# Gate and up products with the weights stationary, so that the hidden values come out transposed

## What is computed

```python
def h_bitlinear(x, w):
    xq = act_quant(fwht(x))      # per-token scale 127 / max|.|, rounded
    wq = weight_quant(w)         # -1, 0, 1 times one scale
    return jnp.einsum('bsh,oh->bso', xq, wq)
gate = h_bitlinear(hidden_states, w_gate)     # 512 -> 2048
up = h_bitlinear(hidden_states, w_up)         # 512 -> 2048
return h_bitlinear(jax.nn.silu(gate) * up, w_down)   # 2048 -> 512
...
x = x + _L0_xattn_ref(_layernorm(x, axis=-1), ...)
x = x + _L0_ffn_ref(_layernorm(x, axis=-1), ...)
```

## Time and profile before

| | |
|---|---|
| median of 3 runs | 1400.6 us (1399.08 to 1401.05) |
| profiled execution, its time | 1399.5 us |
| its span in the trace | 1397.7 us |
| PE busy | 1375.2 us, 98% of the span |
| DVE, ACT, POOL busy | 936.5, 938.9, 449.5 us |
| feed-forward part | from about 1012 us to the end |
| starts of the 13 gate and up groups | 1022.30, 1051.39, then 29.17 apart until 1343.05, last 1371.80 |

### The profile page before, as it was taken

One profiled execution on the slowest core, in us unless ns is written; L12 is line 12 of the kernel. 1 busy time (PEld: TensorE's weight loads), 2 busy tenths in 40 slices (PEclk: granted clock), 3 DMA queues, 4 the chain that ended last, 5 costly groups with the idle time before them and its releaser, 6 DMA issues. The chain is left out here.

```text
span 1397.7 us, 25965 instructions
## 1 busy us (share of the span) xinstructions
PE 1375.2 (98%) x8419; PEld 1181.4 (85%) x8419; DVE 936.5 (67%) x2403; ACT 938.9 (67%) x2072; POOL 449.5 (32%) x325
## 2 busy tenths in 40 slices
PE   9999999999999999999999999999999999999998
PEld 9889868999999999999999999998866677766775
DVE  5312047777777777777777778777466777767775
ACT  5556668888888888888888888888534334343332
POOL 1034314312211212212221222224444555645551
PEclk9999999999999999999999999999999999999999
DMA  8867823334444434443444433435453222232211
GB/s 250 238 181 200 223 75 97 101 106 124 133 120 116 138 110 125 120 133 113 125 122 127 135 109 114 117 99 168 133 155 87 68 61 69 71 96 69 61 31 42
DMA packets 186394, 166.22 MB, mean 119 GB/s; under 512 B 87938, under 2 KB 155540, under 8 KB 184468
## 3 DMA queue, kind: packets, MB, share of 16 engines
q1 hardware_dynamic: 178980, 151.50, 38.4%
q10 hardware_dynamic: 7280, 13.06, 3.6%
HBM read 124.57 MB, written 33.02 MB: 113 GB/s over the span
## 5 line engine op out<-in xcount | busy, mean ns | idle before, releaser
L804 POOL TENSOR_TENSOR rk_sp<-ms_sp,neg_half 124x6 f32<-124x6 f32 x128 | 169.8, 1346 | 615.1 <-DMA ms_sp<-ms 615.1
L1028 ACT ACTIVATE pr<-ex,ri 100x361 f32<-100x361 f32 x256 | 153.6, 600 | 68.5 <-DVE ri L1228 68.5
L1240 DVE CUSTOM_DVE_ANT_0 sc<-psS,rk 100x361 f32<-100x361 f32 x256 | 136.5, 533 | 79.8 <-PE psS L879 63.9
L1021 ACT ACTIVATE ex<-sc,nb,rq_all 100x361 f32<-100x361 f32 x256 | 176.0, 688 | 2.0 <-DVE nb L1249 1.9
L907 PE MATMUL psZ<-pT_hi,cK_hi 120*128 120x400 f32 (+1 forms) x384 | 132.7, 345 | 0.0
L907 PE MATMUL psZ<-pT_hi,cK_lo 120*128 120x400 f32 (+1 forms) x384 | 132.1, 344 | 0.0
L907 PE MATMUL psZ<-pT_lo,cK_hi 120*128 120x400 f32 (+1 forms) x384 | 131.9, 343 | 0.0
L892 PEld LDWEIGHTS psP<-ident,pr 100*120 100x120 f32 (+1 forms) x768 | 73.0, 138 | 46.1 <-issue 35.3
L1228 DVE RECIPROCAL ri<-rs 100x1 f32<-100x1 f32 x256 | 41.3, 162 | 89.5 <-ACT ex L1021 85.5
L1220 DVE TENSOR_TENSOR pT_lo<-psP,pT_hi 122x600 fp32r<-122x600 f32 x128 | 99.1, 774 | 1.5 <-ACT pT_hi L1052 1.3
L922 PE MATMUL psNV<-z,wv_sb 128*128 128x200 f32 x504 | 97.2, 336 | 0.8 <-issue 0.8
(11 more groups left out here) (303 smaller groups left out, 3947.6 us busy)
## 6 DMA issues: line engine op xcount, KB each, us to landing
rk<-rk_dram SPq DMA_DIRECT2D x128, 290.6 KB
q_dram<-q_out SPq DMA_DIRECT2D x64, 200.0 KB, 4.5
q_in<-q_dram SPq DMA_DIRECT2D x64, 200.0 KB, 3.9
o_dram<-o SPq DMA_DIRECT2D x64, 200.0 KB, 4.4
stage<-in_w_ff SPq DMA_DIRECT2D x12, 1024.0 KB, 6.5
w_in<-in_w_ff ACTq DMA_DIRECT2D x48, 256.0 KB, 3.8
o_in<-o_dram SPq DMA_DIRECT2D x12, 1024.0 KB, 6.0
cT_in<-in_ctxT SPq DMA_DIRECT2D x15, 361.0 KB, 4.4
```

Source lines behind the costliest of these rows:

```text
L804: nc.gpsimd.tensor_tensor(rk_sp[:, cols], ms_sp[:, cols], neg_half[0:HG * SKR, :].to_broadcast([HG * SKR, n]), op=ALU.pow).then_inc(g_rk, 1)
L1021: nc.scalar.activation(ex[:, h % 2, :], sc[:, h % 2, :], ACT.Exp, bias=nb[:, h % 2:h % 2 + 1], scale=factor(n), accum_out=rs[:, h % 2:h % ...
L1028: nc.scalar.activation(pr[:, h, SKP - SK:SKP], ex[:, h % 2, :], ACT.Copy, scale=ri[:, h % 2:h % 2 + 1]).then_inc(a_pr, 1)
L1240: nc.vector.tensor_tensor_reduce(out=sc[:, h % 2, :], in0=psS[0:SQ, 0:SK], in1=rk[:, u % 2, h, 0:SK], scale=1.0, scalar=-3.0e38, op0=ALU.m ...
```

## The change

The gate and up products are turned round: the weights `wt` (128x128 of them) are stationary and `q1T` streams with 128 columns, so that the features come out on partitions and the tokens along the row. A block j takes 64 such products instead of 8, first the 32 of gate, then the 32 of up, each half with a semaphore of its own (`p_gate`, `p_up`). `hidden_T` goes. A token's scale is no longer a value per partition: DVE writes it as 128 equal columns (`alpha_rows`), PE transposes that (`al_T`), ACT copies it to `alT`, DVE multiplies gate with it (`gate`), and ACT takes the silu of the result in SBUF. The scale of up is left out of the hidden values and put into `scales2` (`al_up`).

Other edits: the second half of integers (`ints2(i, 1)`) comes behind the first gate block of the next tile; `out_proj` is split into `out_high` (two products per head) and `out_low` (one per head, last), and 12 heads' high products are issued a step ahead rather than 6 heads' whole ones; `norm_T` and `al_T` write `psT`, not `psA`; DVE's `rotate_within`, POOL's steps, the residual's copies on POOL and the last difference of `rotate_across` are cut and placed anew; `high_hT` and `low_hT` read SBUF; the down weights have a semaphore of their own (`d_down`); the count of `busy` products and their places change; the last tile uses the same code with 64 columns, with `rotate_quarters` and `cross_halves` in place of its transposes.

```diff
-        AHEAD, FIRST = 6, 10
+        AHEAD, FIRST = 12, 8
...
-            sp.dma_start(wt[:, 2, :, :].bitcast(BF16), wt_dram[2 * WC:3 * WC].rearrange("c p n -> p c n")).then_inc(d_wt[1], 16)
+            sp.dma_start(wt[:, 2, :, :].bitcast(BF16), wt_dram[2 * WC:3 * WC].rearrange("c p n -> p c n")).then_inc(d_down, 16)
...
+            def rotate_within(t, n):
+                pool.wait_ge(v_h, t * NB + n + 1)
+                if due(t * NB):
+                    pool.wait_ge(v_hT, t * NB)
+                for k, op in enumerate((ALU.add, ALU.subtract)):
+                    nc.gpsimd.tensor_tensor(half_rot[:, n, k * HB:(k + 1) * HB], hid[:, n, 0:HB], hid[:, n, HB:], op=op
+                                            ).then_inc(g_pair0, 1)
...
-                nc.gpsimd.tensor_tensor(half_rot[:, 2:4, :], hid[:, 0:2, :], hid[:, 2:4, :], op=ALU.subtract).then_inc(g_r2, 1)
+                nc.gpsimd.tensor_tensor(half_rot[:, 3, :], hid[:, 1, :], hid[:, 3, :], op=ALU.subtract).then_inc(g_r2, 1)
...
+            def al_T(t):
+                pe.wait_ge(v_scale[0], 6 * t + 6)
+                if due(t):
+                    pe.wait_ge(a_alT, t)
+                nc.tensor.transpose(psT[0][:, 0:TT], al_rows[:], ident[:]).then_inc(p_alT, 1)
...
-                for k in range(2):
-                    for c in range(DC):
-                        last = nc.tensor.matmul(psB[:, 2 * (j % 2) + k, :], q1T[:, c, :],
-                                                wt[:, k, c, j * DIM:(j + 1) * DIM], start=(c == 0), stop=(c == DC - 1))
-                last.then_inc(p_gu, 1)
+                width, chunks = (TH, FC // 2) if last_tile(t) else (TT, FC // NB)
+                for k, done in enumerate((p_gate, p_up)):
+                    for i in range(chunks):
+                        col = (j * chunks + i) * P
+                        for c in range(DC):
+                            last = nc.tensor.matmul(psB[:, 2 * (j % 2) + k, i * width:(i + 1) * width], wt[:, k, c, col:col + P],
+                                                    q1T[:, c, 0:width], start=(c == 0), stop=(c == DC - 1))
+                    last.then_inc(done, 1)
...
                 for j in range(NB):
                     if real(i + 1):
                         gate_up(i + 1, j)
-                if real(i + 2):
-                    out_proj(i + 2, range(FIRST if isinstance(i, int) and i == -1 else AHEAD, H))
-                if real(i + 1):
-                    hidden_T(i + 1, 0)
-                    hidden_T(i + 1, 1)
+                if isinstance(i, int) and i == -1:
+                    first_out_proj(range(FIRST, H))
+                    busy(psT[1], 8)
+                elif real(i + 2):
+                    out_high(i + 2, range(AHEAD, H))
+                    out_low(i + 2)
                 if real(i):
                     down(i, 0, front)
                     down(i, 1, front)
                 if real(i + 1):
-                    rotate_hidden(i + 1, 0)
-                    hidden_T(i + 1, 2)
-                    rotate_hidden(i + 1, 1)
-                    hidden_T(i + 1, 3)
+                    for n in range(NB):
+                        rotate_hidden(i + 1, n)
                 if real(i + 2):
                     norm_T(i + 2)
-                if real(i + 1):
-                    rotate_hidden(i + 1, 2)
-                    rotate_hidden(i + 1, 3)
+                if real(i + 3):
+                    out_high(i + 3, range(0, 3))
+                elif i == TILES - 3:
+                    busy(psA, 5)
                 if real(i + 2):
                     rotate_in(i + 2)
                 if real(i + 3):
-                    out_proj(i + 3, range(0, 4))
+                    out_high(i + 3, range(3, 9))
...
                 if real(i + 2):
                     q1_T(i + 2)
                 if real(i + 3):
-                    out_proj(i + 3, range(4, AHEAD))
+                    out_high(i + 3, range(9, AHEAD))
...
+                if real(i + 2):
+                    al_T(i + 2)
...
-                    nc.scalar.activation(sil[:, j % 2, :], psB[:, 2 * (j % 2), :], ACT.Silu, scale=al[:, 0:1]
-                                         ).then_inc(a_sil, 1)
+            def silu(t, j):
+                act.wait_ge(v_g, t * NB + j + 1)
+                nc.scalar.activation(sil[:, j % 2, :], sil[:, j % 2, :], ACT.Silu).then_inc(a_sil, 1)
...
+            def alpha_rows(t):
+                dve.wait_ge(v_scale[0], 6 * t + 5)
+                nc.vector.tensor_scalar(al_rows[:], w127[:, 0:1].to_broadcast([P, TT]), am[:, 0:1], None, ALU.mult
+                                        ).then_inc(v_scale[0], 1)
...
+            def gate(t, j):
+                dve.wait_ge(p_gate, t * NB + j + 1)
+                dve.wait_ge(a_alT, t + 1)
+                width = TH if last_tile(t) else TT
+                blocks = DIM // width
+                nc.vector.tensor_tensor(sil[:, j % 2, :].rearrange("p (i t) -> p i t", t=width),
+                                        psB[:, 2 * (j % 2), :].rearrange("p (i t) -> p i t", t=width),
+                                        alT[:, 0:width].unsqueeze(1).to_broadcast([P, blocks, width]), ALU.mult).then_inc(v_g, 1)
...
-                nc.vector.scalar_tensor_tensor(hid[:, j, :], psB[:, 2 * (j % 2) + 1, :], al[:, 1:2], sil[:, j % 2, :],
-                                               ALU.mult, ALU.mult).then_inc(v_h, 1)
+                nc.vector.tensor_tensor(hid[:, j, :], psB[:, 2 * (j % 2) + 1, :], sil[:, j % 2, :], ALU.mult).then_inc(v_h, 1)
```

More of the change, by code:

```diff
@@ L1509, in step @@
             def step(i):
+                if i > -2:
+                    if 0 <= i and not last_tile(i):
+                        pool.wait_ge(v_q[1], 2 * i + 2)
+                    move_residuals(i - 1)
                 if real(i + 1) and not last_tile(i + 1):
+                    for n in range(2):
+                        rotate_within(i + 1, n)
                     rotate_pair0(i + 1)
@@ L1514, in step @@
                     inverse_deviation(i + 2)
-                if real(i + 3) and not (isinstance(i, int) and i == -2):
+                if real(i + 3) and i > -2:
                     low_o(i + 3)
[L1517 to L1520, removed]
+                if real(i) and not last_tile(i):
+                    result(i)
             pipeline(pool, step, 3)
@@ L1525, in _, with first_out_proj @@
         def _(pe):
[L1526 to L1531, removed]
+            def first_out_proj(heads):
                 for h in heads:
-                    if first:
-                        pe.wait_ge(v_o, h // OH + 1)
+                    pe.wait_ge(v_o, h // OH + 1)
                     hi, lo = (w[h // HALF][:, h % HALF, :] for w in (wo_hi, wo_lo))
@@ L1540, in out_proj, with out_high, out_low @@
                     last.then_inc(p_out, 1)
+            def out_high(t, heads):
+                if heads[0] == 0:
+                    pe.wait_ge(a_o, t + (NO - 1))
+                    pe.wait_ge(v_x1, t - 1)
+                for h in heads:
+                    for w in (wo_hi, wo_lo):
+                        nc.tensor.matmul(psA[:], o_hi[:, h, :], w[h // HALF][:, h % HALF, :],
+                                         start=(h == 0 and w is wo_hi), stop=False)
+            def out_low(t):
+                pe.wait_ge(g_o, t - 1)
+                for h in range(H):
+                    last = nc.tensor.matmul(psA[:], o_lo[:, h, :], wo_hi[h // HALF][:, h % HALF, :],
+                                            start=False, stop=(h == H - 1))
+                last.then_inc(p_out, 1)
             def norm_T(t):
                 pe.wait_ge(v_xr, t * 2)
+                pe.wait_ge(a_alT, t)
                 for c in range(DC):
-                    last = nc.tensor.transpose(psA[:, c * P:(c + 1) * P], xr[:, c * P:(c + 1) * P], ident[:])
+                    last = nc.tensor.transpose(psT[0][:, c * P:(c + 1) * P], xr[:, c * P:(c + 1) * P], ident[:])
                 last.then_inc(p_xT, 1)
@@ L2025, in step @@
                     scales2(i + 1)
-                    ints2(i + 1)
+                    ints2(i + 1, 0)
                     return
                 if real(i + 1):
-                    for n in range(3):
+                    for n in range(NB):
+                        gate(i + 1, n)
+                        if n == 0 and real(i):
+                            ints2(i, 1)
                         hidden(i + 1, n)
                     rotate_within(i + 1, 2)
-                    hidden(i + 1, 3)
                     rotate_within(i + 1, 3)
@@ L2044, in step @@
                     ints1(0)
+                    alpha_rows(0)
                     return
@@ L2049, in step @@
                     low_hT(i + 1, 0)
+                    rotate_third(i + 1)
+                    low_hT(i + 1, 1)
+                if real(i + 2):
+                    statistics(i + 2)
+                if real(i + 1):
+                    low_hT(i + 1, 2)
+                    low_hT(i + 1, 3)
```

281 lines of the change are left out of this document (122 added, 159 removed).

## The result

The changed kernel takes 1385.68 us (median of 4 runs, 1384.35 to 1386.21), the kernel before 1400.76 (4 runs, 1399.08 to 1401.05): an estimated ratio of 0.9895, 95% interval 0.9883 to 0.9907 (the two medians alone give 0.9892). The forecast was 1387 within 1381 to 1402. The profiled execution is 1386.21 us, span 1384.4.

The account below looks back on a forecast made before the run. PE's queue, busy 29.15 of 29.17 us, was the bound. From 1399.5: first start -1.4, eleven periods -11.1, last but one -1.35, end +0.5, together -13.4, gives 1386.1; with the median's 1.1, 1387 us, range 1381 to 1402.

Parts of the forecast that it names:

- 27.6 without waits: PE's work in a middle tile: 29.17 - 1.74 - 0.2 + 0.11 + 0.23 us.
- The pair of load and product: Gate and up group on PE: each weight load with its 128-column product takes 0.0555 us, the group 7.10 us.
- Rival 5: Gate and up on PE: each pair takes more than 0.069 us; at 0.085 the kernel is slower, 1432 us; chance 0.15.
- The two waits: PE in a middle tile: 0.1 us lost ahead of rotate_in and 0.35 ahead of q1_T, no other wait.
- rival 2: Middle tile: no wait left, POOL's collision doesn't happen, period 27.6 us, kernel 1381 us; chance 0.08.
- The walked chain: One tile from its gate and up start: hidden block 3 ends near 9.35 us, DVE's rotation 13.4, first low part 15.2.
- Rival 3: DVE's chain: later by 0.5 to 0.8 us, PE waits for the third low part, period 28.8, kernel 1394; chance 0.17.
- Rival 4: One-element steps of scales1 also wait behind POOL's low_o and result: period 29.5 us, kernel 1402, no change; chance 0.07.
- DVE's busy time: DVE in a middle tile: from 21.39 us to some 25, less what POOL's blocking gives back.
- The last but one: Last but one tile: no low_o, so the integers' collision goes; 27.4 us against 28.75, -1.35.
- The end: Last tile, 64-column products at 0.035 us each: rotate_hidden at +10.8 us against 10.29, +0.5 (0 to +2.5).
- The first tile: First tile: group starts about 1.4 us earlier, PE waits 0.6 and some 0.8, clock 1.00, period 28.1 against 29.09.

Follow-up runs that it names:

- e6_transposes: Changed kernel with sixteen unread identity transposes added ahead of each tile's down product but the last: 1400.12 us, 1.0005 of the kernel before.
- e7_both: Changed kernel with POOL's result waiting for the integers and four heads' high products instead of three ahead of rotate_in: 1377.0 us, 0.9845 of the kernel before.
- e8_product_earlier: Changed kernel with four heads' high products instead of three ahead of rotate_in, POOL's result left in place: 1379.16 us, 0.9856 of the kernel before.
- e1_result_late: Changed kernel with POOL's result waiting in addition for the integers of width 512: 1380.29 us, 0.9871 of the kernel before.
- e2_dve_more: Changed kernel with one unread 512-column DVE sum added ahead of rotate_across in each tile: 1400.09 us, 1.0009 of the kernel before.
- e9_dve_more_behind: Changed kernel with one unread 512-column DVE sum added behind DVE's part of rotate_across: 1397.74 us, 0.9991 of the kernel before.
- the repeat: Changed kernel unaltered, measured again beside three of its variants on the same chip: 1382.82 us, 0.9887 of the kernel before.
- e4_no_busy: Changed kernel without the eight unread products ahead of the first tile's rotation: 1384.6 us, 0.9888 of the kernel before.
- e5_before_busy: Kernel before with ten unread products put into its first tile's wait: 1398.8 us, 0.9996 of the kernel before.

## Why the prediction was right, point by point

**PE's queue is the bound, and what leaves it is gained.** Right, by e6_transposes. The sum (27.6 without waits) measured 27.46, in e7_both and e8_product_earlier, where almost no wait is left: gate and up +0.31 (7.18 against 6.87, I had +0.23), `al_T` +0.11 as said, so what went is 29.17 + 0.42 - 27.46 = 2.13, where I had 1.94. The sixteen transposes are 1.75 of it at 0.109 each, as said (e6_transposes). The rest is 0.38, where I had 0.2 for the wait of the loads. I have no run that splits it. About 0.2 of it stands in the output projection, for which I had nothing: 30 products took 7.17 between gate and up and `hidden_T`, 24 take 1119.85 - 1114.26 = 5.59 now, and six more at 0.23 would make 6.97.

**The pair of load and product, 0.0555.** Right: 0.056 over all 128. The rule of the Trainium skill ("TensorE: Matmul & The Clock Gate", section "Back-to-back issue gap"), about 81 ns for each pair, does not hold here; by it the group would have taken an estimated 10.4 us, not 7.18. Rival 5 is out.

**The two waits.** Right in place: `rotate_in` 0.19 (0.1 said), `q1_T` 0.25 (0.35 said), together 0.44 where 0.45 to 0.5 was said. No other wait stands in the middle tile. POOL's part in the second, 0.15 of the 0.25, is shown by e1_result_late; rival 2, which had no collision, is out.

**The walked chain.** Hidden block 3 ended 9.39 behind T (9.35 said), DVE's rotation 13.3 (13.4), the first low part 15.0 (15.2). Its thin slacks are real: e2_dve_more and e9_dve_more_behind turn 0.6 us of DVE into 1.2 to 1.4 of the period. Rival 3 named the right danger, and the change stayed 0.2 short of it. The moved integers hide where I put them; `copy_alT` took 0.28 (0.3 taken).

**One-element steps beside POOL.** They kept 0.15 to 0.21 under `low_o` and `result`. Rival 4 is out.

**DVE's busy time.** Said some 25 less what the blocking gives back, measured 22.40. The gates cost their 2.7. But two operations that took 2.40 beside POOL in the earlier trace rows now run between two POOL instructions, among the four in 1.42: 1.7 us of before was waiting. The remaining 0.8 below my sum I have not traced.

**Where it was off.** The mechanism held; three terms of the sum were mis-sized. The period used was 28.15, it is 27.94: 0.14 from PE's sum above, the rest from waits rounded up; over eleven, 2.3 us too little gained. The last but one gained 0.70, not 1.35: I let POOL's collision end with `low_o`, but it moved to another operation. This is DVE's timeline of the changed kernel there.

```profile
1348.86 1.51 DVE L1863 TENSOR_SCALAR xn<-x,mv,rstd 128x512 f32<-128x512 f32 x1
```

POOL's:

```profile
1348.72 1.37 POOL L1509 TENSOR_TENSOR y<-y,x 128x512 f32<-128x512 f32 x1
```

PE's, where `norm_T` waits:

```profile
1351.22 0.66 PE L1564 MATMUL psT<-ident,xr 128*128 128x128 f32 x4 [0.59 <-DVE xr L1871]
```

Without `low_o` in its queue POOL does the result early and meets the layer norm's operation, 1.51 instead of 0.55; with the result held back this tile takes 27.25 (e1_result_late), near the 27.4 I had. The end was +0.03, not +0.5: PE's timeline has the 64-column products and the last `rotate_hidden`:

```profile
1358.47 3.89 PE L1617 MATMUL psB<-q1T,wt 128*128 128x64 bf16 x128
...
1368.83 0.38 PE L1639 MATMUL psB<-had,hT_hi 128*128 128x256 f32 x1 [1.31 <-DVE hT_lo L1839]
```

The products start 0.029 apart in the mean (0.035 taken), and `rotate_hidden` comes 10.36 behind T, not 10.8. With the 0.07 of the first start these come to 2.1 us more gain than the 13.4 forecast. In the first pair of profiles the 2.14 us by which the part ahead happened to end later hid just that. The medians do not depend on that one execution: they gained 15.1 us in the first comparison and 15.8 in the repeat, against 13.6 said (1400.6 to 1387). So the forecast was 1.5 to 2.2 us short, and it is partly luck that it was no more, since the last but one tile and the periods err in opposite directions. One slip of bookkeeping: the chances listed with the rivals add up to 0.10 for no change and 0.15 for slower, not to 0.08 and 0.17.

**The first tile** started its group 1.33 earlier (1.4 said), waited some 0.3 and 0.5 us (0.6 and 0.8 said) and kept full clock. What I thought of its clock afterwards was too much: I expected 2 to 3 us from it in e4_no_busy and e5_before_busy and found 0.8 and nothing.

## What to carry to other kernels

Where PE's queue is full, making the weights the stationary side and streaming the activations, 128 columns at a time, cost 0.31 us a tile here, and it paid because it spared 1.75 us of transposes behind it; cost it by the pitch of the nearest products in the trace, even of four. Then walk the other engines in order up to each place where PE wants something, and look for slack in tenths: here a move of one DVE operation was worth 1.0 us a tile, one of 0.6 added cost twice itself. Last, fill the waits that are left with work that stands behind them in the same queue: moving two products was worth 0.4 us a tile, more than the 0.14 of removing the cause of one wait.

## What the runs showed that I had not expected

- Pairs of a 128x128 weight load and a 64-column product took 1362.20 - 1358.47 = 3.73 us for 128 of them, 0.029 each, half of the 128-column pitch: down to that distance the load sets no floor here.
- A DVE operation of 512 or 1024 elements between SBUF operands that was asked for beside a POOL instruction waited until that had ended (2.29 for 1.23, 1.76 for 0.69, 1.51 for 0.55, 0.94 for 0.42), and POOL waited for DVE in the same way (2.32 for 1.28). An operation that reads PSUM (the sum of `x`, 0.68) and one-element steps (0.15 to 0.21) did not. So the sum of `x` was free under POOL's difference, and it stopped being free once another operation stood ahead of it (e9_dve_more_behind).
- Leaving out the products that nobody reads brought a wait of 2.03 us and 3 us at half clock behind it, and cost 0.84 us in all (e4_no_busy): a mean granted clock of 0.94 in that tile looks worse than it is.
